# Two-block transformer kernel, first block: the twelve weight chunks issued from ScalarE's DMA queue instead of SP's

## What is computed

```python
x = x + L0(x, cond)      # masked attention over the 256 columns, 8 heads of 16, q = k = v = x^T Wq^T; then Wo
x = x + L1(x, cond)      # norm, modulation by cond @ ada_w, attention with 16 heads of 128, out_w, norm, ffn with gelu
```

## Time and profile before

| | |
|---|---|
| median of 3 runs | 802.7 us (802.21 to 804.07) |
| the profiled execution | 802.39 us |
| its span | 800.6 us, 1.8 us less than its time |
| PE / PEld busy | 747.2 us (93%) / 615.9 us (77%) |
| DVE / ScalarE / POOL busy | 385.5 / 436.6 / 144.8 us |
| first block | about 0 to 204 us of the span |
| DMA queue q1 | 75.01 MB, 35.1% of 16 engines' span |

### The profile page before, as it was taken

One profiled execution on the slowest core, in us unless ns is written; L12 is line 12 of the kernel. 1 busy time (PEld: TensorE's weight loads), 2 busy tenths in 40 slices (PEclk: granted clock), 3 DMA queues, 4 the chain that ended last, 5 costly groups with the idle time before them and its releaser, 6 DMA issues.

```text
span 800.6 us, 12914 instructions
## 1 busy us (share of the span) xinstructions
PE 747.2 (93%) x4737; PEld 615.9 (77%) x4737; DVE 385.5 (48%) x782; ACT 436.6 (55%) x1189; POOL 144.8 (18%) x136
## 2 busy tenths in 40 slices
PE   3689999997699999999999999999999999899997
PEld 2555555554598888888888888888888888778886
DVE  1155666666234543444545444545444345545444
ACT  1056776765357454555564555565544566647553
POOL 4133444200033111111111111111111122200000
PEclk9999999999899999999999999999999999999999
DMA  6999988740433221221221221212222223220001
GB/s 196 244 155 188 200 206 192 138 64 1 131 119 103 69 80 68 66 79 67 67 80 66 66 75 59 76 66 65 79 80 66 80 93 105 80 79 31 29 21 53
DMA packets 68851, 75.69 MB, mean 95 GB/s; under 512 B 4040, under 2 KB 48064, under 8 KB 68800
## 3 DMA queue, kind: packets, MB, share of 16 engines
q1 hardware_dynamic: 68800, 75.01, 35.1%
HBM read 47.96 MB, written 27.03 MB: 94 GB/s over the span
## 4 chain that ended last, share of the span: by engine, by line
PE 69%; DVE 3%; ACT 2%; DMA 1%; issue 0%; DVEq 0%; SPq 0%; ACTq 0%
PE bank L672 27%; PE pair L672 14%; PE ring L672 13%; PE ring L958 7%; PE pair L944 6%; PE ring L116 1%; DVE x1l L1186 1%; ACT x1h L1046 1%; PE ring L977 0%; ACT probs L1065 0%; DMA x1f<-in_L_cond_ffn_w_dram 0%; PE ring L913 0%; DVE ol L1219 0%; DVE pB L1197 0%; DMA turned<-pB 0%
## 5 line engine op out<-in xcount | busy, mean ns | idle before, releaser
L1065 ACT ACTIVATE probs<-pair,nm 128x128 f32<-128x128 f32 x256 | 98.5, 486 | 183.1 <-DVE nm L1208 183.1
L1321 POOL TENSOR_TENSOR probs<-probs,rinv 128x512 f32<-128x512 f32 x64 | 66.7, 1042 | 356.6 <-DVE rinv L1216 356.6
L672 PE MATMUL bank<-x1h,w_hi 128*128 128x512 f32 x256 | 112.1, 438 | 5.6 <-DVE x1l L1186 5.5
L602 DVE TENSOR_REDUCE mx<-ring 128x2 fp32r<-128x512 f32 x128 | 80.1, 683 | 64.2 <-PE ring L401 64.2
L672 PE MATMUL bank<-x1l,w_hi 128*128 128x512 f32 x256 | 101.5, 396 | 0.0
L672 PE MATMUL bank<-x1h,w_lo 128*128 128x512 f32 x256 | 101.2, 395 | 0.0
L539 ACT ACTIVATE pt<-ring 128x512 f32<-128x512 f32 x128 | 70.1, 594 | 44.2 <-PE ring L413 44.0
L1239 DVE COPY Vv<-pair 128x512 f32<-128x512 f32 x64 | 44.2, 691 | 80.4 <-PE pair L672 80.4
L672 PE MATMUL pair<-w_hi,x1l 128*128 128x256 f32 x256 | 72.7, 284 | 0.0
L672 PE MATMUL pair<-w_lo,x1h 128*128 128x256 f32 x256 | 72.4, 283 | 0.0
L672 PE MATMUL pair<-w_hi,x1h 128*128 128x256 f32 x256 | 72.2, 282 | 0.0
(11 more groups left out here) (175 smaller groups left out, 1476.0 us busy)
## 6 DMA issues: line engine op xcount, KB each, us to landing
turned<-pB SPq DMA_DIRECT2D x63, 256.0 KB, 2.0
pT<-turned SPq DMA_DIRECT2D x63, 256.0 KB, 2.8
QS<-qd SPq DMA_DIRECT2D x16, 384.0 KB
stage<-in_L_cond_qkv_w_dram SPq DMA_DIRECT2D x12, 512.0 KB, 7.6
qd<-qh SPq DMA_DIRECT2D x16, 256.0 KB
KS<-qd SPq DMA_DIRECT2D x16, 256.0 KB
mb<-in_cond_dram SPq DMA_DIRECT2D x8, 256.0 KB, 10.4
qd<-ql SPq DMA_DIRECT2D x8, 256.0 KB
```

Source lines behind the costliest of these rows:

```text
L602: dve.tensor_reduce(mx[:, 2 * b + s, :], ring[:, 2 * b + s, :].rearrange("p (k q) -> p k q", k=2), AX_X, ALU.max, negate=True).then_inc(dv ...
L672: last = nc.tensor.matmul(bank, w(k), x(k), start=(start and i == 0), stop=(stop and i == len(terms) - 1))
L1065: last = nc.scalar.activation(plain(probs)[:, t] if direct else probs[:, :, b, :].rearrange("p c a -> p a c"), Sb[:, t] if direct else Sb[ ...
L1321: pool.tensor_tensor(w, w, r, ALU.mult).then_inc(pool_p, 1)
```

## The change

`weights(c)` moves from SP's program to ScalarE's, with the same waits and the same transfers. Chunks 0 and 1 are issued right after the copy of `wq_h`, ahead of `queries(0)`. Chunk n // 2 + 2 is issued in each odd unit n up to 19, behind `exponentials(n, 0)`. ScalarE's wait for `pool_lo` of 2(c - 1) = n + 1 means there that `w_lo` of the unit n itself is done.

```diff
--- before.py
+++ after.py
@@ -279,13 +279,6 @@
                             r = 64 * s + r * DK
                             sp.dma_start(dst[r:r + n * DK, g % 2, :, :].bitcast(F32),
                                          v[s, DK * c:DK * (c + n)]).then_inc(l_q[g % 2], 16)
-
-                def weights(c):
-
-                    if c >= 2:
-                        sp.wait_ge(pool_lo, 2 * (c - 1))
-                    k, n = divmod(c, 3 * INNER // CHUNK)
-                    sp.dma_start(stage[:, c % 2, :], qkv_v[:, k, n * CHUNK:(n + 1) * CHUNK]).then_inc(l_st[c % 2], 16)
 
                 sp.dma_start(X[:, 0:2, :], x[0:2].rearrange("b p d -> p b d")).then_inc(l_x0, 16)
                 mask(0)
@@ -310,8 +303,6 @@
                 sp.dma_start(X[:, 4:B, :], x[4:B].rearrange("b p d -> p b d")).then_inc(l_x, 16)
                 mask(2)
                 gather(1)
-                weights(0)
-                weights(1)
                 for g in range(NGR):
                     if g + 1 < NGR:
                         spread(g + 1)
@@ -319,9 +310,6 @@
                         mask(g + 3)
                     if g + 2 < NGR:
                         gather(g + 2)
-                    for c in (2 * g + 2, 2 * g + 3):
-                        if c < CHUNKS:
-                            weights(c)
 
             @block.gpsimd
             def _(pool):
@@ -514,6 +502,16 @@
                 act.wait_ge(pe_wT, 1)
                 nc.scalar.copy(wq_h[:, :], tbank[:, 0:P]).then_inc(act_set, 1)
 
+                def weights(c):
+
+                    if c >= 2:
+                        act.wait_ge(pool_lo, 2 * (c - 1))
+                    k, n = divmod(c, 3 * INNER // CHUNK)
+                    act.dma_start(stage[:, c % 2, :], qkv_v[:, k, n * CHUNK:(n + 1) * CHUNK]).then_inc(l_st[c % 2], 16)
+
+                weights(0)
+                weights(1)
+
                 def queries(g):
 
                     wait(act, pe_q, g + 1)
@@ -574,6 +572,8 @@
                                        stage[:, n // 2 % 2, n % 2 * 512:n % 2 * 512 + 512]).then_inc(act_hi, 1)
                     if n < UNITS:
                         exponentials(n, 0)
+                    if n % 2 == 1 and n // 2 + 2 < CHUNKS:
+                        weights(n // 2 + 2)
                     if n == UNITS - 4:
                         act.wait_ge(pool_x, NGR)
                         act.wait_ge(l_q[(NGR - 1) % 2], LQ * (NGR // 2))
```

## The result

The changed kernel took 800.37 us at the median of 20 runs (lowest 797.25), the kernel before 803.54 us at the median of 20 runs. The ratio is 0.9951, 95% interval 0.9933 to 0.9968: 3.9 us faster, between 2.6 and 5.4. A second batch of 12 runs gave 0.9954 (0.9935 to 0.9973). One of the twenty executions took 2485 us; neither median nor ratio hangs on it. The kernel before measured 803.54 here and 802.7 at the median of the three runs shown before the change; the forecast of 800.2 was counted from the latter.

What follows compares the result with a forecast made beforehand. The first block was priced, by what waits for chunk transfers hold up: +0.1 - 2.1 - 1.45 + 0.6 + 0.3 = -2.5 us on the profiled 802.39; from the 802.7 median, 800.2 us, range 797.0 to 805.5.

Steps and rivals of the forecast that it cites:

- Step 1: Start: early chunks from ScalarE end the exponentials' wait for chunk 0, gaining 2.5 us if first scores stay at 30.33.
- Step 2: Start: two early chunks delay the `qd` copies and first scores by 2.6 us; net of the start +0.1.
- Step 3: SP's program: without twelve chunk issues and the waits for POOL, the next spread leaves about 1.2 us earlier.
- Step 4: Steady groups: chunk waits at units 4, 8, 16 and 20 go, -2.1 (with the slow clock) and -1.45 us.
- Step 5: Units 8 to 19: an even chunk now falls beside the spread at 1.3 us, giving back 0.6 us.
- Step 6: ScalarE's ten loop issues, 0.56 us each at the median, before second exponentials: cost 0.3 us, bounds 0 and 3.0.
- Rival C: Loop: ScalarE's issue waits for SP's simultaneous spread issue, becoming 1.16 us, costing 0.45 in five units; 802.2, chance 0.18.
- Rival A: Start: early chunks delay the `qd` copies not at all or only partly, -2.5 us more, 797.7; chance 0.14.
- Rivals B and D: B: transfers bind, chunk inside spread costs 3 to 4 us, 807, chance 0.16; D: unit 4's slow clock stays, 801.8, 0.10.

Runs made afterwards that it cites:

- x1: Kernel before with only chunks 0 and 1 moved to ScalarE, the other ten staying with SP; ratio 0.9965 (0.9942 to 0.9989).
- x2: Changed kernel, but chunks 0 and 1 stay with SP behind gather 1, the other ten issued by ScalarE; ratio 0.9979 (0.9956 to 1.0001).
- x7: Changed kernel, but ScalarE issues chunks 0 and 1 behind queries(1), beside the spread; ratio 0.9986 (0.9957 to 1.0015).
- x4: Changed kernel plus an unread load of 0.377 MB in units 6, 10, 14 and 18; ratio 0.9979 (0.9942 to 1.0017).
- x5: Kernel before, all chunks in SP's queue, reordered: chunks 0, 1 behind the modulation weights, each later even chunk ahead of its turn's gather; 799.99 us, ratio 0.9951.
- x9: SP's queue alone in x5's order, but only chunk 0 early, chunk 1 behind gather(1); 798.19 us, ratio 0.9935.
- x8: Kernel before with x5's loop order and, in unit 0, first exponentials ahead of the w_hi copy; ratio 0.9948 (0.9924 to 0.9972).
- x10: Kernel before with one edit: in unit 0 the first exponentials go ahead of the w_hi copy; 806.44 us, ratio 1.0034.
- x6: SP's queue alone in x5's order, but chunks 0 and 1 behind gather(0); median 802.60 us, ratio 0.9983 (0.9955 to 1.0012).

## Why the prediction was right, and where its parts were not

The time was within 0.2 us of the forecast of 800.2. The gain was 3.9 us (2.6 to 5.4) where 2.5 was forecast, since the kernel before measured 0.8 slower over twenty runs than over three. The parts were less good than the sum.

- **Step 1, ScalarE's side of the start (2.5 us): right.** The exponentials follow the modulations at once, and the two early issues cost nothing.
- **Step 2, delay by the early chunks: right in kind, 2.6 us taken, 0.9 measured at the spread.** Two things were wrong in it. The landing of `qd` moved by 1.4 and not 2.6, against "the strip leaves no hole on the busy half". And the spread wasn't waiting for that landing: 18.13, read as SP's wait, is the end of SP's own issues (the last two start at 16.93 and take 1.16), which hid another 0.5 of the delay. The net of the start is not +0.1 but about -1.8: from issue of `qd` to first exponentials the two profiles of before took 30.4 and 30.7, the changed kernel 28.2 and 29.4. In the times it is x1's 0.35% against x2's 0.21%, which the two intervals don't tell apart.
- **Step 3, SP: right that spreads leave earlier.** The one of unit 7 leaves at 76.21, 1.57 us ahead of the second exponentials of that unit (77.78); before it was 0.40 (79.70 and 80.10). That is 1.2 us earlier, as taken.
- **Step 4, steady waits: mechanism right, size from one execution.** All four waits went, and groups are 18.8. Chunk 2 landed at 56.7, 11.2 us behind its issue at 45.5, and not by 55 "at worst", but still in time. But "-2.1 with the slow clock" holds for the profiled execution only; the second profile of before lost nothing there. The loop's share is 2.2 by the mean of two profiles, 1.7 by x2's ratio (with an interval down to nothing), against 3.55 forecast.
- **Step 5, a chunk beside the spread: mis-sized.** 1.3 us taken, 2.1 measured in x7. The +0.6 did not come. The slack before unit 4 had been 1.5, but grew to 4.4 and 5.1, and lasted for the few groups that have chunks, but for 0.2 us in one profile (x4 shows it run out).
- **Step 6, ScalarE's issues: right, and less than taken.**

```profile
L510 ACTq DMA_DIRECT2D stage<-in_L_cond_qkv_w_dram x12: 334/334/550, 7.6 to 133.4; - x12
```

The issue takes 0.33 us (two early ones 0.98 together), not 0.56; the idle time before the second exponentials is unchanged. 0 instead of +0.3. The 0.56 wasn't SP's price either, but the middle between its 0.33 and the 1.2 to 1.3 of those issued right behind a gather; in x5 and x9, where they stand elsewhere, SP's median is 0.35. Rival C is refuted in this kernel: ScalarE's issue at 77.01 lies within SP's two of 76.21, and neither took longer than alone (0.33 and 1.23). In x7 (18.70 and 18.78) ScalarE's two took 0.87. The block that the Trainium skill has two issuers share (Perfetto Trace Analysis, "DMA Instruction — HWDGE (DVE, Sync)") may exist, but costs nothing to see here.

Rival A, early chunks free, was two thirds right. The Trainium skill says that transfers of all issuers run on the same 16 engines and interleave, so that a second issuer saves only the time of issuing (DMA: Bandwidth & Descriptors, "Issuing engines are not separate DMA queues"). That agrees with x5, where one queue gives the same time, 799.99, and with x7, where the chunks on ScalarE's queue made the spread 4.3 us longer. Rivals B and D did not happen in the changed kernel, but both mechanisms exist: x4, x8 and x10 show them. Not in my sum at all was the spell at the end of the block (+1.1 in both profiles of the changed kernel). The errors, -1.9 at the start, +1.3 in the loop (3.55 less 2.2), -0.9 in the two costs that did not come, +1.1 behind the block, largely cancelled: with them the sum is -2.9, and the mean spans of the two profiles each differ by 2.7. The forecast was partly lucky.

What stays open: what decides whether the clock falls in the gap at the end of the block and when it rises at the start, why x9 is fastest, and x6's ratio.

## What to carry to other kernels

Before a transfer is moved to a second queue, move it within the first: here the order gave the whole gain. Price an early transfer by what it delays on the chain that sets the start, and see first whether that chain waits for the transfer or for the issuing queue. Look where compute that comes earlier will next meet a transfer that doesn't: taking some 2 us off the start alone made the kernel 2.7 us slower (0.8 to 4.7). And take two profiles of a kernel before building a sum on one group's length, or on a lead of a microsecond at the start.

## What the runs showed of the hardware

- Short waits of PE and ScalarE (0.9 to 3 us) were followed by 3.4 or 6.8 us at a granted clock of 0.5, the 1.2 GHz level, in some places and not in others (before: a spell behind the wait of 1.41 us, none behind 0.75, 0.66 and 0.70). Behind unit 4 such a spell and its wait together made the group 20.9 to 24.1 us instead of 18.8 (before, x8, x10); the second profile of before had neither.
- The same 2.73 us gap of PE at the end of the block went with a fall in six profiles and not in seven others, and what follows unit 27 was some 1.1 us longer where it did. The gap of 5.02 us a little later went with a spell of half clock in all fourteen.
- At the start the granted clock rose 7.5 (x8) to 13.1 us (changed) behind the first exponentials, 10.3 and 13.0 in two profiles of the kernel before. Between 10.3 and 13.0 lie 1.2 us at unit 3.
- A copy of 0.52 MB to all partitions cost 2.1 us beside the spread, whose transfers go to few rows at 110 to 170 GB/s. Ahead of the `qd` copies, which run at a DMA share of about 0.5, it cost their landing 0.7 to 1.1, and the spread's issue 0.4 to 0.8.
- An issue of a chunk took 0.33 us on ScalarE's queue and 0.35 on SP's (medians, x5 and x9 for SP); SP's issues right behind the three copies of a gather took 1.2 to 1.3.
